# Attention 1 of a two-layer block: turning the softmax probabilities with VectorE's 32x32 blocks and a bounce through DRAM

## The reference

```python
qkv = hidden_states @ w_qkv                                   # (8, 128, 512) @ (512, 6144)
scores = jnp.einsum('bqhgd,bkhd->bhgqk', q, k) * scale
attn = jax.nn.softmax(scores + bias[None], axis=-1)           # ALiBi bias, causal
out = jnp.einsum('bhgqk,bkhd->bqhgd', attn, v).reshape(B, S, NH * D)
return out @ w_o                                              # (4096, 512)
```

## Time and profile before

| | |
|---|---|
| time, median of 3 runs | 2028.7 us (2025.08 to 2028.84) |
| the profiled execution's own time | 2021.16 us |
| its span in the trace | 2018.5 us |
| PE, DVE, ACT, POOL busy | 97%, 76%, 65%, 47% of the span |
| DMA traffic | 142.21 MB, mean 70 GB/s |

### The profile page before, as it was taken

How to read it: one execution, slowest core, us unless ns; L and a number is a source line. 1 busy time by engine, 2 the same in 40 slices (tenths; PEclk the granted TensorE clock), 3 DMA queues, 4 the chain that set the end, 5 groups by cost and what they waited for, 6 DMA issues and landing times.

```text
span 2018.5 us, 35965 instructions
## 1 busy us (share of the span) xinstructions
PE 1966.2 (97%) x12221; PEld 1669.4 (83%) x12221; DVE 1536.3 (76%) x3386; ACT 1317.0 (65%) x3796; POOL 940.4 (47%) x917
## 2 busy tenths in 40 slices
PE   7999999999999999999999999999999999999997
PEld 6777777888888888888888888888888888888774
DVE  6777765667666656688887887888878878888997
ACT  4676773545544545567777777777777777777785
POOL 3200014565665665644544544545445445454662
PEclk9999999999999999999999999999999999999999
DMA  7301102333433334412121121121211211212010
GB/s 263 100 28 48 54 1 82 118 100 95 140 96 97 123 102 77 129 42 82 32 64 53 33 84 32 32 84 32 64 53 33 84 32 32 84 33 84 29 31 37
DMA packets 91158, 142.21 MB, mean 70 GB/s; under 512 B 24914, under 2 KB 63058, under 8 KB 86498
## 3 DMA queue, kind: packets, MB, share of 16 engines
q1 hardware_dynamic: 69474, 89.55, 13.4%
q0 software_dynamic: 21504, 50.37, 8.7%
HBM read 119.93 MB, written 19.93 MB: 69 GB/s over the span
## 4 chain that ended last, share of the span: by engine, by line
PE 85%; DVE 7%; ACT 4%; DMA 2%; issue 2%; SPq 0%; POOL 0%; ACTq 0%; DVEq 0%
PE PS L1721 9%; PE PS L1733 9%; PE PS L1633 8%; PE PS L1499 8%; PE PS L1556 8%; PE PS L1706 6%; PE PS L1688 6%; PE PS L1647 4%; PE PS L1512 4%; PE PS L1691 3%; PE PS L345 3%; PE PS L1527 3%; PE PS L1542 2%; PE PS L501 1%; PE PS L1657 1%
## 5 line engine op out<-in xcount | busy, mean ns | idle before, releaser
L1304 POOL DMA_INDIRECT ffn_weights<-in_kcache,arena x256 | 259.8, 1015 | 78.0 <-issue 77.1
L2626 POOL DMA_INDIRECT vcache<-in_vcache,rows x256 | 249.9, 976 | 77.1 <-issue 55.6
L2475 ACT ACTIVATE pr<-pr,sm 128x640 f32<-128x640 f32 x256 | 209.4, 819 | 64.6 <-DVE sm L2085 64.4
L2101 DVE TENSOR_TENSOR prT_lo<-PS,prT_hi 128x512 fp32r<-128x512 f32 x320 | 208.8, 685 | 42.0 <-ACT prT_hi L2486 25.4
L2486 ACT ACTIVATE prT_hi<-PS 128x512 fp32r<-128x512 f32 x320 | 178.0, 597 | 67.9 <-PE PS L1706 67.8
L2085 DVE CUSTOM_DVE_ANT_0 pr<-PS,ffn_weights,sm 128x640 f32<-128x640 f32 x256 | 211.0, 878 | 0.5 <-PE PS L1691 0.5
L2632 POOL TENSOR_TENSOR vcached_lo<-vcache,vcached_hi 128x512 fp32r<-128x512 f32 x64 | 83.3, 1301 | 235.8 <-ACT vcached_hi L2457 235.8
L1706 PE MATMUL PS<-consts,pr 128*128 128x128 f32 x1280 | 172.1, 273 | 1.4 <-DVE prT_lo L2101 1.2
L1706 PEld LDWEIGHTS PS<-consts,pr 128*128 128x128 f32 x1280 | 149.6, 141 | 25.2 <-DVE prT_lo L2101 1.9
L1688 PE MATMUL PS<-kT_hi,qT_hi 128*128 128x320 f32 x512 | 155.2, 311 | 3.8 <-DVE sm L2085 2.4
L1688 PE MATMUL PS<-kT_lo,qT_hi 128*128 128x320 f32 x512 | 154.1, 309 | 0.0
(11 more groups left out here) (324 smaller groups left out, 6446.3 us busy)
## 6 DMA issues: line engine op xcount, KB each, us to landing
arena<-in_wqkv SPq DMA_DIRECT2D x16, 1536.0 KB
arena<-in_wo SPq DMA_DIRECT2D x16, 1024.0 KB
turned_keys<-ffn_weights POOLq DMA_DIRECT2D x64, 256.0 KB
kcache<-turned_keys SPq DMA_DIRECT2D x256, 64.0 KB
arena<-in_wcT SPq DMA_DIRECT2D x8, 1024.0 KB, 6.4
ffn_weights<-in_kcache,arena POOLq DMA_INDIRECT x256
vcache<-in_vcache,rows POOLq DMA_INDIRECT x256
arena<-in_xT SPq DMA_DIRECT2D x8, 256.0 KB, 7.8
```

The costliest lines, as they stand in the source:

```text
L1304: pool.indirect_dma_start(out=key_pages[:, n % 2, c, :], out_offset=None, in_=T["kcache"], in_offset=bass.IndirectOffsetOnAxis(ap=key_rows ...
L2101: dve.tensor_tensor(prT2[1][:, n % 3, :, :].rearrange("p h n -> p (h n)"), bank(4 + n % 2), prT2[0][:, n % 3, :, :].rearrange("p h n -> p ...
L2475: act.activation(pr2[:, h, :], pr2[:, h, :], ACT.Exp, bias=nm2[:, h:h + 1], scale=-1.0, accum_out=rs2[:, h:h + 1]).then_inc(a2_ex, 1)
L2626: pool.indirect_dma_start(out=vcache[:, c, :], out_offset=None, in_=T["vcache"], in_offset=bass.IndirectOffsetOnAxis(ap=rows[:, g, b, c:c ...
```

## The change

For items 8 to 54 (`TURNED`) PE's `turn_probs1` is gone. In its place DVE turns the item's probabilities by 32x32 blocks from SBUF to SBUF (one instruction), SP stores the 256 KB to a DRAM buffer, waits for that store, and loads them back with four DMAs of 64 KB, each filling 32 partitions with four runs of 512 bytes for each partition. The high part is then made by ACT and the low part by DVE from this landed tile in the next step, PE's `weigh1` follows a step later as well, and the output product two steps later. v needs a third buffer slot for that. The landed tile holds the queries in another order (a, h, n of 32 instead of h, n of 128), which the copies of the attention's output undo.

SP's order is written anew: group weights come in pieces (four q parts of 256 KB, one k/v part of 512 KB, four output parts of 256 KB), placed behind the bounce of particular items; unit loads stand two steps ahead of where their data are first read, no longer behind a 1 MB transfer. The high parts of the output weights are made one step later. The low parts of the probabilities stand ahead of `add1` on DVE, and `hi_of_probs1` of the previous item stands ahead of `kT_copy1` on ACT.

```diff
+        TURNED = range(B, ITEMS - B - 1)
...
+        def delayed_out1(i):
+            return (i - 1,) if i - 1 not in TURNED else (i - 2,) if i - 2 in TURNED else ()
...
+            def load_q_weights1(g, parts=range(GH)):
+                for r in parts:
+                    wait(sp, a1_wl, QPARTS * (g - 1) + r + 1)
+                    sp.dma_start(stage_qkv[:, :, r * P:(r + 1) * P],
+                                 T["wqkv1"][g, :, :, r * P:(r + 1) * P]).then_inc(a1_w, 16)
...
+            def bounce_probs1(i):
+                sp.wait_ge(a1_pT, i + 1)
+                kept = probs_kept[i - TURNED[0], :, :, :]
+                sp.dma_start(kept.rearrange("p c n -> p (c n)"),
+                             probs_turned.rearrange("p c h n -> p (c h n)")).then_inc(stored1(i)[0], 16)
+                sp.wait_ge(a1_pTl, i)
+                sp.wait_ge(*stored1(i))
+                for c in range(4):
+                    sp.dma_start(probs_landed[32 * c:32 * (c + 1), :].rearrange("p (a n) -> p a n", a=4),
+                                 kept[:, c, :].rearrange("(a j) n -> j a n", j=32)).then_inc(landed1(i)[0], 16)
...
+            for i in TURNED:
+                bounce_probs1(i)
+                g, b = group_of(i)
+                if b == 0 and 1 <= g < 5:
+                    load_units(2 * g - 2)
+                elif b == 1:
+                    if g + 2 < G:
+                        load_q_weights1(g + 2, (0,))
+                    if 2 <= g < 6:
+                        keep_units(2 * g - 4)
+                elif b in (2, 3, 4):
+                    load_out_weights1(g + 1, ((0,), (1,), (2, 3))[b - 2])
+                elif b in (5, 6) and g + 2 < G:
+                    load_q_weights1(g + 2, ((1, 2), (3,))[b - 5])
+                elif b == 7 and g + 2 < G:
+                    load_kv_weights1(g + 2)
...
-                project_out1(i - 1)
+                for n in delayed_out1(i):
+                    project_out1(n)
...
-                turn_probs1(i)
+                if i not in TURNED:
+                    if i - 1 in TURNED:
+                        weigh1(i - 1)
+                    turn_probs1(i)
                 if i + 1 in AHEAD:
                     scores1(i + 1)
...
+                if i in TURNED:
+                    project_q_head(n, (1,))
+                    if i - 1 in TURNED:
+                        weigh1(i - 1)
+                    project_q_head(n, (2,))
...
+            def turn_probs1(i):
+                dve.wait_ge(a1_n, i + 1)
+                if i - 1 in TURNED:
+                    dve.wait_ge(*stored1(i - 1))
+                dve.transpose(probs_turned.rearrange("p c h n -> p h c n"),
+                              pr1(i).rearrange("p (h c n) -> p h c n", h=GH, c=4)).then_inc(a1_pT, 1)
...
             def hi_of_probs1(i):
-                act.wait_ge(a1_pT, i + 1)
-                act.activation(prT2[0][:, i % 2, :, :].rearrange("p h n -> p (h n)"), bank(4), ACT.Copy).then_inc(a1_pTh, 1)
+                if i in TURNED:
+                    act.wait_ge(*landed1(i))
+                    act.wait_ge(a1_pv, i - 1)
+                else:
+                    act.wait_ge(a1_pT, i + 1)
...
+                if i - 1 in TURNED:
+                    hi_of_probs1(i - 1)
                 if i + 1 in AHEAD:
                     kT_copy1(i + 1)
```

More of the change, by code:

```diff
@@ L262, in build @@
         s_w0 = [sem(f"w{n}0_loaded") for n in ("q", "k", "v", "o_then_ffn_out")]
-        s_wc = [sem(f"adapter_loaded{i}") for i in range(2)]
+        s_wc = [sem(f"adapter_then_{what}_loaded{i}") for i, what in enumerate(("turned_probs1", "kv_weights1"))]
         s_wh0, s_wl0 = sem("weights0_hi"), sem("weights0_lo")
@@ new lines, in load_kv_weights1, with load_out_weights1 @@
+            def load_kv_weights1(g):
+                wait(sp, a1_wl, QPARTS * g)
+                sp.dma_start(stage_qkv[:, :, GH * HD:QKV], T["wqkv1"][g, :, :, GH * HD:QKV]).then_inc(s_wc[1], 16)
+            def load_out_weights1(g, hs=range(GH)):
+                wait(sp, a1_wol, GH * g)
+                for h in hs:
+                    sp.dma_start(stage_out[:, h, :], T["wo1"][g, :, h, :]).then_inc(a1_wo, 16)
+            def bounce_probs1(i):
[8 more added lines that the diff above has]
+                                 kept[:, c, :].rearrange("(a j) n -> j a n", j=32)).then_inc(landed1(i)[0], 16)
@@ L1596, in step1 @@
                     project_q(1, (0, 1, 2))
-                weigh1(i)
+                if i not in TURNED:
+                    if i - 1 in TURNED:
+                        project_out1(i - 1)
+                    weigh1(i)
                 if i == GH:
@@ L1926, in step1 @@
                     lo_of_x(i - FROM_X)
+                if i - 1 in TURNED:
+                    lo_of_probs1(i - 1)
                 if i == ITEMS - 2:
@@ L1941, in step1 @@
                 else:
-                    add1(i - 1)
+                    for n in delayed_out1(i):
+                        add1(n)
                     lo_of_v1(i + 1)
-                    lo_of_probs1(i)
+                    if i not in TURNED:
+                        if i - 1 in TURNED:
+                            lo_of_o1(i - 1)
+                        lo_of_probs1(i)
                 if b < GH and 0 < g < G - 1:
                     lo_of_weights1(g + 1, b)
+                new_out = g > 0 and b == (1 if i - 1 in TURNED else 0) and i != TURNED[0]
                 if i + 1 == ITEMS - 1:
@@ L2391, in step1 @@
                     hi_of_weights1(g + 1, b)
-                if b == 0 and g > 0:
+                if g > 0 and b == (1 if i - 1 in TURNED else 0) and i != TURNED[0]:
                     for h in range(GH):
                         hi_of_out_weights1(g, h)
-                hi_of_o1(i)
+                if i not in TURNED:
+                    hi_of_o1(i)
+                elif i - 1 in TURNED:
+                    hi_of_o1(i - 1)
                 if head_of(i) < ITEMS:
```

86 lines of the change are left out of this document (57 added, 29 removed).

## The result

Four runs of the changed kernel took 2009.76 to 2011.78 us, median 2010.22; four of the kernel before, taken beside them, took 2025.08 to 2028.84, median 2027.22. The ratio is 0.9916, with a 95% interval of 0.9899 to 0.9933: 17.0 us faster. The profiled execution of the changed kernel took 2009.76 us (span 2008.0). That of the kernel before, 2021.16, was faster than all four timed runs, so from profile to profile only 11.4 us are gone.

What follows compares the result with a forecast made beforehand. PE, busy 97% of the span, was taken as the bound. Terms -20.2 - 1.2 + 1.4 = -20.0 us gave ratio 0.990, or 2008.6 us on the runs' median; forecast range 2005 to 2014 (0.70), 8 in 10 within 2004 to 2020.

Steps and rivals of the forecast that it cites:

- PE's turns: Four turns of probabilities leave PE in each of 47 items, 0.43 us each time: 20.2 us gained.
- DVE's turn hidden: DVE's new turn, 0.60 to 0.70 us per item, ends at +4.3 in the step, hidden by 1.5 us of slack.
- The bounce: Probabilities' store to DRAM and loads back: 2.0 + 3.3 + 0.2 = 5.5 us, 2.9 less than the limit of 8.4.
- The two rules: Skill rules against the bounce: transposing loads 19 times slower, 63 us; HBM latency under load, 1.8 us more on each half.
- The stall of item 34: PE's single wait, before item 34's turns, caused by a late feed-forward weight load, goes: -1.2 us.
- The start: Step 9, without an output product on PE: PE waits for k's copy and a few tenths for the high part, +1.4 us.
- The end: Step 55, where PE has two output products and two `weigh1`: 0, at most +1 us.
- Keys: DVE's wait for a key's store or gather once a group: 0, at most +1 us in each of 6 groups.
- Rival C: DVE's in-order waits add up in some steps of each group: +6 to +9 us; with A, in part, 0.15.
- The sum: All terms together: -20.0 us against the profiled 2021.16, giving 2001.2, ratio 0.990.
- Rivals A and B: Bounce length T grows under load: A shrinks the gain (2019 at 8.8); B, slower than before (2047 at 10), chance 0.08.
- the formula: Step length P = (8.97 + T) / 2 for bounce length T above 8.4 us; gain gone at T = 9.2.

Runs made afterwards that it cites:

- dead_bounce: Kernel before with the new load order, plus the bounce's DMAs from constants, nobody but SP waiting for them; 2027.29 us, 1.0022 of before.
- double_turn: Changed kernel with DVE's turn of the probabilities done twice; 2004.23 us, 0.9917 of before.
- second profile: Changed kernel unaltered, run and profiled again in a later batch; 1999.19 us, 0.9879 of before.
- pieces_only: Kernel before with weights in pieces and the new load order, no bounce, turns still on PE; 2027.35 us, 1.0021 of before.
- no_bounce: Changed kernel without each item's store and four loads, the turned blocks read where DVE left them (output wrong); 2007.54 us, 0.9922 of before.
- third profile: Changed kernel unaltered, run and profiled a third time in the last batch; 2005.30 us, 0.9919 of before.
- whole_weights: Changed kernel with later groups' weights loaded in one piece each, 1.5 MB and 1 MB; 2008.53 us, 0.9928 of before, a sixth run left out.
- two_stores: Changed kernel with the turned probabilities stored twice in series before the loads; 2051.71 us, 1.0154 of before.

## Why the prediction was right, and where it was not

**The time** (2008.6; 2010.22 measured) and the ratio (0.990; 0.9916, then 0.9879 and 0.9919) are inside the range. That 2010.22 lies so near 2008.6 is partly luck: profile to profile the first pair gained 11.4 us, the three gains by medians are 17.0, 24.0 and 16.9 where 20 was forecast, and the 24.0 stands beside a profile whose steps gained 18.8. Those 5 us are not explained, as that batch has no profile of the kernel before. By its own steps:

- *PE's turns, 47 x 0.43 = 20.2 us.* Right: a plain step went from 9.09 to 8.66 in every profile. In `dead_bounce`, where PE keeps the turns and has the new order of loads and the bounce's traffic, it stays 9.09; the turns are the gain.
- *DVE's turn hidden.* Right: 0.71 us each, DVE's busy time +31.6 in the first profile and +28.8 in the second (forecast 31). It ended at +4.0, 0.3 earlier than I had it, and `double_turn` shows that 0.75 more would cost 3 us in all and not 35.
- *The bounce, 5.5 us against a limit of 8.4.* The mechanism was right and both sizes were off to the worse: 6.25 us in the median of the second profile (6.3 and 6.5 in the others, where some landings have no record) against a limit of about 8. From store to loads it took 2.5 for my 2.1 (an output store in a quiet stretch and a wake-up of 0.1, for which I had no row; SP's issue of the store follows the turn by 0.03), the loads 3.7 for my 3.3. The slack is some 1.6 us and not 2.9, and single items use it up: 26 in the second profile cost 1.3 us. I had counted nothing for the tail.
- *The two rules.* The loads took 3.7 us, not 63. The Trainium skill (VectorE: DVE Perf Modes, The three transpose paths) states its 19 times against the hardware's transposing DMA, for a copy whose innermost destination stride is large. I had left out that condition and multiplied another base, these loads themselves; they move whole runs, and no run here times either of the copies that the page compares. The two halves took 0.4 us each more than my rows of quiet stretches, at 167 GB/s. The Trainium skill (DMA: Bandwidth & Descriptors, Latency and other measured facts) gives 2 us of latency at high load; my estimate of 1.8 more on each half did not come, but the page doesn't say what load is high, so this isn't a test of it.
- *The stall of item 34, -1.2.* It went; 1.45 measured in `pieces_only`, where the turns stay on PE.
- *The start, +1.4.* Step 9 lasts 7.15 us for 5.87 of work in two profiles, 1.3; 7.86 in one. `no_bounce` has the same 7.15, so the stall is k's copy alone; the few tenths that I gave to the high part aren't seen.
- *The end, 0 to 1.* Step 55 has an output product (2.80) and a `weigh1` (0.69) more than 9.09, 12.58; it took 12.57 to 12.96.
- *Keys, 0.* DVE's waits for keys in these steps fell from 10.9 us (8.8 for stores, 2.1 for a gather) to 1.8, 0.8 and 0.4. Rival C didn't come.
- *The sum.* -20.0 forecast; -18.8 and -17.7 in steps 8 to 56 of the second and third profile. The terms I had not: late bounces (0 to 1.3 in a profile) and late signals of PE (0 to 10).

Rivals A and B had the right mechanism: `whole_weights` pays 1.2 to 2.0 us at T = 8.9 to 9.7, and `two_stores` is slower than before at T = 10.2. There B was too mild: at T = 10 it said 18 us above the kernel before, and `two_stores` is 30.0 above its own. That its 2047 lies near 2051.71 is chance, since the kernel before took 2028.7 in the one case and 2021.67 in the other. Two of my remarks were wrong by my own numbers. A store or loads of twice the length would not have reached the 9.2 us at which the gain is gone: twice the store gives T = 7.5, twice the loads 8.8; it takes both growing, from the measured 6.25 by half as much again (and to 8.9, if the limit is 8). And at T = 9.1 the formula leaves 3 us of the gain and not 2.

## What to carry to other kernels

Where one engine is busy all the time, a transfer through DRAM can take work off it at next to no cost, as here, if it has a whole step to arrive; what it cost here came not from the mean time but from the tail, so keep large loads out of the queue ahead of it (in pieces, behind the loads and ahead of the next store) and count the engines that work in order between landing and use. When a DMA order is rewritten, follow also the small transfers that moved with it: here a 4 KB store in a new place cost more than the pieces gained. When you compare a variant with a forecast in absolute microseconds, compare differences to the kernel before of the same batch. And when the change moves a few microseconds, profile it more than once: the first profile of this kernel lost some 10 us to late signals; the second lost none to them and the third under 3.

## What the runs showed of the hardware

- 12 MB out and 12 MB back, on top of 105 GB/s, didn't lengthen one plain step of PE (9.09 both times, `pieces_only` and `dead_bounce`).
- Behind a 4 KB store to DRAM in runs of 4 bytes, 14 to 38 packets of 4096 bytes of the gathers took 1.5 to 8.9 us each, where the median is 0.2; in `pieces_only` DVE waited 7.56 us for a gather.
- A 256 KB store took 2.2 to 3.0 us (once 4.6) when a weight piece or unit load had been issued 2.9 us or more before it, and 3.0 to 4.9 with less than 2 us between them (`two_stores`).
- Behind a 1.5 MB load the same store took 5.3 to 6.2 us (`whole_weights`).
- In the first and the last batch, signals of PE's products came up to 4.9 us later than their records, in profiles that also lack records of signals; in the eight profiles of the other two, never more than 0.4, and none is missing.
- The kernel before timed 2021.7 to 2027.2 us (medians of four batches), and the gain of the change was 17.0, 24.0 and 16.9 us; the intervals of the second and the others don't meet.
